# Splitting the key transfers of the 8x8 window stage over two issuing engines, and rotating before normalising

## The reference, cut to what matters

```python
xw = x.reshape(B, H // WH, WH, W // WW, WW, C).transpose(0, 1, 3, 2, 4, 5).reshape(-1, N, C)
qkv = xw @ qkv_w.T + qkv_b
q = _rope2(q.reshape(-1, WH, WW, hd)).reshape(-1, NH, N, hd)      # x1 * cos - x2 * sin, x1 * sin + x2 * cos
k = _rope2(k.reshape(-1, WH, WW, hd)).reshape(-1, NH, N, hd)
attn = jax.nn.softmax(q * scale @ jnp.swapaxes(k, -2, -1), axis=-1)
out = (attn @ v) ...
return out @ proj_w.T + proj_b
```

## Time and profile before

| | us |
|---|---|
| median of 3 runs (lowest to highest) | 2614.84 (2593.13 to 2616.89) |
| the profiled execution, its own time | 2611.62 |
| its span | 2609.8 |
| TensorE busy in the span | 1993.9 |
| VectorE busy | 1362.4 |
| ScalarE busy | 1059.0 |
| mean granted clock of TensorE | 0.833 of full |

### The profile page before, as it was taken

The page is one execution under the profiler, slowest core; times in us unless marked ns, Lnnn a source line. Parts: engine busy times, 40 slices in busy tenths (PEclk is TensorE's granted clock), DMA queues, the critical chain, the costliest instruction groups (busy, mean ns, idle before and its releaser), DMA issues.

```text
span 2609.8 us, 98500 instructions
## 1 busy us (share of the span) xinstructions
PE 1993.9 (76%) x37794; PEld 1494.9 (57%) x37794; DVE 1362.4 (52%) x3822; ACT 1059.0 (41%) x1826; POOL 451.5 (17%) x416
## 2 busy tenths in 40 slices
PE   2888888866588888888777877777777777777777
PEld 1655666544466666666555555555555555555555
DVE  2444444457444444444355556555566555665555
ACT  0222222223222222222245555555555555555555
POOL 2000000024222332332111111111111111111110
PEclk9777777778799999999878787788877888877888
DMA  2000000024433333333100000000000000000000
GB/s 90 20 19 16 16 17 16 16 62 103 95 91 96 92 93 96 92 92 95 44 9 9 11 9 10 9 9 10 10 10 9 9 9 11 10 9 9 9 11 6
DMA packets 221125, 94.80 MB, mean 36 GB/s; under 512 B 171090, under 2 KB 207762, under 8 KB 220818
## 3 DMA queue, kind: packets, MB, share of 16 engines
q1 hardware_dynamic: 221074, 94.08, 14.8%
HBM read 62.74 MB, written 18.42 MB: 31 GB/s over the span
## 4 chain that ended last, share of the span: by engine, by line
issue 34%; PE 21%; SPq 19%; DVE 12%; POOL 8%; ACT 3%; DVEq 1%; POOLq 0%; DMA 0%; ACTq 0%
SPq L391 10%; PE ps_D L761 4%; POOL rstd_ret L455 3%; ACT prob L945 3%; SPq L380 3%; POOL rstd_bin L455 3%; POOL rstd_ffn L455 2%; DVE prob L1168 2%; PE ps_OT L810 2%; PE ps_AV L771 2%; SPq L362 2%; PE ps_T L822 2%; PE ps_J L827 2%; PE ps_OT L811 1%; PE ps_J L817 1%
## 5 line engine op out<-in xcount | busy, mean ns | idle before, releaser
L945 ACT ACTIVATE prob<-ps_D 128x1024 bf16<-128x1024 f32 x512 | 516.5, 1024 | 254.0 <-PE ps_D L761 253.9
L1168 DVE TENSOR_TENSOR prob<-prob,xb 128x1024 bf16<-128x1024 bf16 x512 | 352.5, 689 | 129.2 <-ACT prob L945 123.3
L761 PE MATMUL ps_D<-g,w_parts 128*128 128x256 bf16 x2048 | 365.4, 309 | 4.3 <-ACT prob L945 0.2
L761 PEld LDWEIGHTS ps_D<-g,w_parts 128*128 128x128 bf16 x2048 | 213.5, 114 | 84.8 <-issue 31.7
L1123 DVE TENSOR_REDUCE m_sb<-ps_D 128x4 f32<-128x400 f32 x256 | 135.3, 570 | 209.7 <-PE ps_D L667 194.1
L933 ACT ACTIVATE prob<-ps_D 100x512 f32<-100x512 f32 x256 | 139.0, 595 | 218.3 <-PE ps_D L689 218.3
L771 PEld LDWEIGHTS ps_AV<-pair_sel,prob 128*128 128x128 bf16 x4096 | 185.0, 101 | 70.8 <-DVE prob L1168 47.1
L455 POOL TENSOR_TENSOR rstd_ffn<-veps_ffn,minus_half 128x2 f32<-128x2 f32 x64 | 59.3, 927 | 890.5 <-DVE veps_ffn L995 890.5
L771 PE MATMUL ps_AV<-pair_sel,prob 128*128 128x2 bf16 x4096 | 182.0, 165 | 40.2 <-DVE prob L1168 39.5
L470 POOL TENSOR_TENSOR tile_a<-q_st,q_mask 128x1024 f32<-128x1024 f32 x64 | 123.4, 1927 | 410.6 <-DMA q_st<-q_d 277.1
L503 PE MATMUL ps_T<-ident,xn_f 128*64 128x128 f32 x128 | 38.8, 407 | 196.8 <-DVE xn_f L1007 191.6
(11 more groups left out here) (159 smaller groups left out, 3948.9 us busy)
## 6 DMA issues: line engine op xcount, KB each, us to landing
tile_b<-v_d SPq DMA_DIRECT2D x640, 40.0 KB
key_st<-k_d SPq DMA_DIRECT2D x64, 175.0 KB, 3.0
key_st<-k_d SPq DMA_DIRECT2D x64, 167.0 KB, 3.0
w_exp<-experts SPq DMA_DIRECT2D x64, 129.0 KB, 2.2
k_d<-kpad SPq DMA_DIRECT2D x32, 140.0 KB, 2.3
xin<-in_x SPq DMA_DIRECT2D x32, 128.0 KB, 2.1
tile_a<-rot SPq DMA_DIRECT2D x256, 16.0 KB
q_d<-q_sb SPq DMA_DIRECT2D x32, 128.0 KB, 2.4
```

The lines of the kernel that those rows point to most:

```text
L761: mm = pe.matmul(double[k % 2][:, u * 256:(u + 1) * 256], w_parts[:, (k * 4 + u) * P:(k * 4 + u + 1) * P], g3[:, half, :], start=True, sto ...
L945: act.activation(sgn[:, k % 2, :], double[k % 2][:, :], ACT.Sign).then_inc(BN["sign"], 1)
L1168: dve.tensor_tensor(prod[:, k % 2, :].rearrange("p (u n) -> p u n", u=4), sgn[:, k % 2, :].rearrange("p (u n) -> p u n", u=4), xb2[:, 1 - ...
```

## The change

There are two edits, both in the 8x8 stage. First, SP's `k_in` issues only the transfers of `j` = 0 and 1, four of the eight, and ACT gets a `k_in` of its own with the other four (`j` = 2 and 3). ACT's `k_in` has the same two waits, for the rotation of the strip and for the scores two strips back. It stands at the end of ACT's body i, behind the copy of the turned tokens, and twice in the prologue. Second, in DVE's body i the rotation of strip i+2 stands ahead of the normalising of strip i.

```diff
@@ -317,7 +317,7 @@
             def k_in(i, par):
                 sp.wait_ge(T1["rope"], times(i + 1))
                 sp.wait_ge(T1["scores"], times((i - 1) * 2))
-                for j in range(4):
+                for j in range(2):
                     for e in range(2):
                         sp.dma_start(k_tok[par][32 * j + HD * e:32 * j + HD * (e + 1), e, :],
                                      rot[32 * j + HD * (e + 2):32 * j + HD * (e + 3), par, :]).then_inc(T1["k_in"], 16)
@@ -879,6 +879,14 @@
+            def k_in(i, par):
+                act.wait_ge(T1["rope"], times(i + 1))
+                act.wait_ge(T1["scores"], times((i - 1) * 2))
+                for j in range(2, 4):
+                    for e in range(2):
+                        act.dma_start(k_tok[par][32 * j + HD * e:32 * j + HD * (e + 1), e, :],
+                                      rot[32 * j + HD * (e + 2):32 * j + HD * (e + 3), par, :]).then_inc(T1["k_in"], 16)
+
             def tok(j, par):
@@ -892,10 +900,13 @@
                     tok_v(i + 1, 1 - par)
                 if not last or i + 2 < NT:
                     tok_turned(i + 2)
+                    k_in(i + 2, par)
 
             tok_turned(0)
+            k_in(0, 0)
             tok_v(0, 0)
             tok_turned(1)
+            k_in(1, 1)
             pairs(act, tok)
@@ -1083,9 +1094,9 @@
                     tok_rows(i - 1)
                 if not last or i + 1 < NT:
                     tok_max(i + 1)
-                tok_normalize(i)
                 if not last or i + 2 < NT:
                     tok_rope(i + 2, par)
+                tok_normalize(i)
```

## The result

The changed kernel takes 2743.83 us (median of 4 runs, 2738.2 to 2749.78) against 2613.26 us, 1.051 times as long (95% interval 1.046 to 1.056). The forecast was 2746. Its profiled execution took 2738.2 us, 126.6 more than the one before.

What follows compares the result with a forecast made beforehand. TensorE's work and waits bound the 8x8 stage; 4.32 us more in each of 31 strips is 134, less 2.66 at the start, 131, on 2611.6 gives 2743, plus 3 for the median: 2746 us; range 2680 to 2828.

Steps and rivals of the forecast that it cites:

- The held copy: On ScalarE the copy of the maxima queues behind the rotation wait and four issues, delaying TensorE's scores 4.48 us a strip.
- The issue's price on ScalarE: Each key transfer issued by ScalarE was taken to cost 0.665 us, SyncE's price; bounds from rows were 0.38 and 1.33.
- a cheap issue: Rival, chance 0.10: ScalarE pays 0.38 us per issue, 1.14 us less a strip, 35 in all, giving 2711 us.
- a shared one: Rival, chance 0.18: ScalarE's and SyncE's issues exclude each other, giving 2828 us if fully, 2758 if only for 0.38 us.
- Normalising hidden: VectorE's later normalising ends at 248.8, before the projection at 252.6; without the scores' delay it would be 0.7 us late.
- The clock: TensorE's clock falls in every strip instead of every second, after 5.4 us nearly idle, making each strip 19.68 us.
- the one of 3.21 us: TensorE's idle waiting for keys in the fast strip before the change, taken as enough to make its clock fall.
- the slow strip: The earlier kernel's strip with scores at half clock from 230.13, 11.34 us to the coarse product, taken as every strip's model.
- The start: Four fewer transfers on SyncE land the first strip's keys 2.66 us sooner, cutting its 5.67 us wait by that.
- The other stages: Stages outside the 8x8 one keep their instructions and were predicted not to change.
- The rival of the other side: Rival, chance 0.05: ScalarE isn't held, so only gains remain, 51 us less 10 for late normalising, giving 2574 us.

Runs made afterwards that it cites:

- the eight issues alone: The changed kernel with all eight key transfers issued by ScalarE and none by SyncE: 2831.54 us, ratio 1.089 to the kernel before.
- rotating alone: The kernel before with only the second edit, rotation of strip i+2 ahead of normalising strip i: 2567.26 us, ratio 0.984; timed again, 2567.96 us.
- the split alone: The kernel before with four of the eight key transfers issued by GpSimd, VectorE normalising first as before: 2528.81 us, ratio 0.969.
- the fill: The changed kernel with eight extra, unused TensorE products between the turning of the maxima and the scores: 2697.13 us, ratio 1.037.

## Why the prediction was right

*The held copy.* Right in mechanism and size. Predicted 4.48 us from the reductions' chain: rotation 2.19, 0.12, four issues 2.66, copy to scores 0.42. Measured 2.20, 0.11, 2.63 and 0.42. The chain left out what lies between the last issue and the copy, 0.43 us in the strip shown and 0.04 in the next. The wait of L567 went from 0.46 to 5.30.

*The issue's price on ScalarE*, which no row showed. Taken as SyncE's 0.665; it is 0.66 by the block, as above. The two rivals that hung on it fall: a cheap issue by that row, a shared one by the eight issues alone, which are no shorter. The Trainium skill (Perfetto Trace Analysis, DMA Instruction — HWDGE) has the descriptor generator locked for one sequencer at a time, and by that the time would have been between 2758 and 2828; what the trace shows of it is 0.07 us more per issue on SyncE, off the path, and none on ScalarE.

*Normalising hidden.* Right: it ends at 260.63, the projection starts at 266.98. That it isn't hidden without the delay was shown too: 0.7 us was reckoned, 0.61 measured in strips at full clock and 0.37 with the clock falling.

*The clock.* One fall in each strip and scores at 1.2 GHz were right. The reason given, an idle as long as the one of 3.21 us, is only partly so: rotating alone has no such idle and its clock falls in every strip as well. From strip 0's copy to strip 30's the stage takes 591.2 us (63.11 to 654.32) for 30 strips, 19.7 each, against 19.68 predicted. That it fits so closely is in part luck, for the single strips run from 18.7 to 22.2: the clock comes back 8.5 to 11.6 us behind the start of the scores, 10.3 on the mean, where the slow strip that served as the model had 11.1, and the 0.43 us ahead of every second copy goes the other way.

*The start.* Four transfers less on SyncE were to give 2.66 us at the first strip; its coarse product starts 1.66 sooner (54.35 instead of 56.01). In the prologue ScalarE's four issues (48.92 to 52.13) stand ahead of its copy of the values, too, and TensorE waits 4.99 us for that copy before it turns the next tokens. The first copy of the maxima is 2.5 us later than before, the last 132.9 (668.74 against 535.81), against 131 predicted.

*The other stages.* The span grew by 126.6, so the later stages took 6 us less. No step predicted that. Behind the last copy, where all these kernels have the same instructions, the thirteen profiled executions take 2067.7 us (the change) to 2084.9 (rotating alone), so 6 us is within what this part varies by.

*The rival of the other side* was priced at 2574 for a kernel whose ScalarE isn't held. With GpSimd in its place and both edits that is 2566.56, and the key wait was gone. What the price of 2574 had not seen is the size that the same step can have with the clock up: with the split alone 2528.81.

*What the loss is made of.* Against rotating alone: 93 us by the wait for the rotation, 84 by the four issues. The issues cost what they hold, 2.65 us in each of 31 strips, 82. The wait costs more than the 64 us that it holds (31 times 2.06), for the clock falls earlier in the scores and comes back later.

## What to carry to other kernels

An engine with idle time isn't a free place for a wait: its list is served in order, so ask what stands next behind the wait and who waits for that. Time held ahead of a short copy on the main path can cost more than its length (4.7 us in each of 31 strips would be 146 us), and the wait with its four transfers costs 177 us ahead of that copy, 27 behind it, and nothing on an engine that has no part in the stage. When two edits come together, time each alone: one of these was a gain of 1.6% under a loss of 6.9%.

## What the runs showed of the hardware

- An 8-partition, 16 KB transfer between SBUF tiles costs its issuer, by the median, 0.625 us on SyncE (0.692 while ScalarE issues, too) and 0.632 on ScalarE, with SyncE issuing or not; GpSimd's four took 2.05, 0.51 each. GpSimd started them 0.6 us later than SyncE, which woke on the same rotation.
- ScalarE's first instruction behind its transfers starts 0.04 us after them inside the loop's body (242.71 behind 242.67) and 0.43 later across the loop's end (261.68 behind 261.25).
- TensorE's granted clock fell in the middle of scores that kept it fully busy, where the idle ahead of them was 0.46 us (rotating alone) or 1.5 us (with the fill). In the same kernel, rotating alone, it stayed at 2.4 GHz for 43 us on end in one stretch, and with GpSimd's split for 65 us in strips of 11.8 us with key waits of 0.8 to 1.1.
